# Picking the sixteen stand-in experts of a gate: an eight-largest search with replacement instead of a comparison of all pairs

## The reference, cut to what matters

```python
seq_rep = mean(hidden, axis=1)                 # (16, 512)
affinity = normed(seq_rep) @ normed(sim_matrix)  # (16, 32)
logits = affinity - sigmoid(gates)
gated = relu(logits)
mask = gated > 0
inactive = sum(mask, axis=1) == 0              # a row with no active expert
_, fb_idx = top_k(logits, 16)                  # its sixteen stand-ins
fb_mask = sum(one_hot(fb_idx, 32), axis=1)
mask = where(inactive, max(mask, fb_mask), mask)
routing = softmax(where(mask > 0, gated, -FMAX))
```

## Time and profile before

| | |
|---|---|
| three runs | 1649.87, 1651.27 and 1651.45 us; median 1651.27 us |
| the profiled execution | 1654.6 us, of which its span (first to last instruction) is 1652.9 us |
| PE, DVE, POOL, ACT busy | 92%, 72%, 62% and 59% of the span |
| mean granted TensorE clock | 0.955 of full speed |
| gated mixture block | from 386.3 to 541.5 us of the span |

### The profile page before, as it was taken

How to read it: one execution, slowest core, us unless ns; L and a number is a source line. 1 busy time by engine, 2 the same in 40 slices (tenths; PEclk the granted TensorE clock), 3 DMA queues, 4 the chain that set the end, 5 groups by cost and what they waited for, 6 DMA issues and landing times.

```text
span 1652.9 us, 27994 instructions
## 1 busy us (share of the span) xinstructions
PE 1513.4 (92%) x8637; PEld 1045.7 (63%) x8637; DVE 1194.2 (72%) x1863; ACT 980.0 (59%) x1527; POOL 1032.2 (62%) x855
## 2 busy tenths in 40 slices
PE   4999999997668599999999999886999999999996
PEld 3677777775434344444444444356899999899995
DVE  7688888888637567777777777256777777777774
ACT  6323333333624167888888887745767776677763
POOL 4788888884305478888888887601455555555553
PEclk9999999998879589999999999987999999999998
DMA  7344444446634857777876774292344444444443
GB/s 252 107 135 137 135 136 137 137 140 168 149 90 157 194 128 186 193 189 186 202 187 188 191 193 109 89 343 79 64 78 77 77 77 78 77 77 78 77 77 52
DMA packets 110841, 224.23 MB, mean 136 GB/s; under 512 B 12704, under 2 KB 12704, under 8 KB 109856
## 3 DMA queue, kind: packets, MB, share of 16 engines
q1 hardware_dynamic: 94848, 185.88, 40.0%
q0 software_dynamic: 15904, 37.23, 13.0%
HBM read 146.71 MB, written 75.84 MB: 135 GB/s over the span
## 4 chain that ended last, share of the span: by engine, by line
PE 41%; DMA 19%; issue 3%; DVE 2%; ACT 1%; POOL 1%; SPq 0%; POOLq 0%; DVEq 0%; ACTq 0%
DMA out_rows<-XN,slots 17%; PE pB L1426 10%; PE pO L1436 8%; PE pA L1408 8%; PE pA L1580 4%; PE pO L1449 4%; PE pO L1592 4%; DMA XN<-normed_rows,slots 1%; PE pO L1562 1%; PE pB L1417 1%; PE pA L1570 1%; PE pA L1498 1%; POOL out_rows L1392 1%; DVE low L1772 1%; DMA qs<-q_low 0%
## 5 line engine op out<-in xcount | busy, mean ns | idle before, releaser
L1772 DVE TENSOR_REDUCE low<-pA 128x2 f32<-128x1024 f32 x256 | 307.7, 1224 | 119.8 <-PE pA L1408 105.6
L1665 ACT ACTIVATE pt<-pB 128x512 f32<-128x512 f32 x512 | 287.9, 594 | 93.3 <-PE pB L1426 85.5
L431 PE MATMUL y<-kv,toep 128*128 128x288 f32 x1280 | 327.8, 413 | 9.0 <-DVEq L63 5.8
L1392 POOL DMA_INDIRECT out_rows<-XN,slots x71 | 194.9, 2746 | 215.0 <-DMA out_rows<-XN,slots 171.6
L431 PEld LDWEIGHTS y<-kv,toep 128*128 128x128 f32 x1280 | 239.0, 191 | 97.6 <-DVEq L63 34.1
L1580 PEld LDWEIGHTS pA<-XN,fc 128*128 128x128 f32 x2272 | 265.9, 193 | 8.0 <-issue 2.7
L1580 PE MATMUL pA<-XN,fc 128*128 128x128 f32 x2272 | 266.8, 276 | 1.9 <-issue 1.0
L1426 PE MATMUL pB<-qs,ks 98*128 98x512 f32 x512 | 230.0, 453 | 2.7 <-ACT pt L1665 2.4
L1426 PEld LDWEIGHTS pB<-qs,ks 98*128 98x128 f32 x512 | 97.3, 192 | 192.8 <-ACT pt L1665 147.7
L1408 PE MATMUL pA<-ks,qs 96*128 96x512 f32 x512 | 191.6, 419 | 20.5 <-DMA qs<-q_low 19.0
L401 ACT ACTIVATE ym<-y 128x384 f32<-128x384 f32 (+1 forms) x128 | 52.6, 411 | 230.6 <-PE y L431 230.6
(11 more groups left out here) (281 smaller groups left out, 2388.2 us busy)
## 6 DMA issues: line engine op xcount, KB each, us to landing
ks<-ctx_high SPq DMA_DIRECT2D x64, 256.0 KB, 4.6
qs<-q_high SPq DMA_DIRECT2D x64, 256.0 KB, 6.3
kc<-in_ctx_conv SPq DMA_DIRECT2D x32, 384.0 KB, 5.3
XN<-in_x SPq DMA_DIRECT2D x16, 512.0 KB, 10.5
toep<-kernel_and_skip SPq DMA_DIRECT2D x32, 256.0 KB, 3.6
ct<-in_ctx SPq DMA_DIRECT2D x16, 512.0 KB, 6.4
ctx_high<-kh SPq DMA_DIRECT2D x16, 512.0 KB, 4.5
ctx_low<-kl SPq DMA_DIRECT2D x16, 512.0 KB, 5.1
```

The costliest lines, as they stand in the source:

```text
L431: m = pe.matmul(y[half].rearrange("p (l n) c -> p l n c", l=CB)[:, l, :, 0:PAIRS], toep[u][:, (l - s) * P:(l - s + 1) * P], kv[u][:, half, ...
L1392: pool.indirect_dma_start(out=out["out"], out_offset=bass.IndirectOffsetOnAxis(ap=slots[:, j:j + 1], axis=0), in_=ys[j % 2], in_offset=Non ...
L1665: act.activation(pt[s][:, h, :], bank(u, n), ACT.Exp, scale=SCALE1).then_inc(s_exp, 1)
L1772: dve.tensor_reduce(ap(low[u % 2], t % CB * NH + t // CB, [[NH, 2], [1, 1]]), pA[n % 2], op=ALU.max, axis=AX.X, negate=True).then_inc(s_re ...
```

## The change

The rank of all logits goes. In its place VectorE finds the eight largest of the 32 logits of each row (`max`), replaces these eight in a copy by the most negative number (`match_replace`), and does both once more on the copy. What is then equal to the most negative number is one of the sixteen largest. The tile `later` and its two POOL instructions go with it, and so does its share of `s_con`: PE waits for 4 instead of 5.

```diff
-            later, over, same = (WM[0:B].rearrange("p b k h -> p (b k h)")[:, n * E0 * E0:(n + 1) * E0 * E0]
-                                 .rearrange("p (e f) -> p e f", f=E0) for n in range(3))
+            best = [sb(st, f"best{i}", [B, 8]) for i in range(FALLBACK // 8)]
+            left = [sb(st, f"left{i}", [B, E0]) for i in range(FALLBACK // 8)]
...
-            CONS = 5 + 1 + HQ
+            CONS = 4 + HQ
...
-                pool.memset(later, 1.0).then_inc(s_con, 1)
-                pool.wait_ge(s_con, 5)
+                pool.wait_ge(s_con, 4)
...
-                    pool.wait_ge(s_con, 6 + g)
+                    pool.wait_ge(s_con, 5 + g)
...
-                    if j == 5:
-                        pool.wait_ge(s_ot, j + 1)
-                        pool.affine_select(out=later, in_=later, compare_op=ALU.is_gt, fill=0.0, base=0,
-                                           pattern=[[1, E0], [-1, E0]], channel_multiplier=0).then_inc(s_con, 1)
-                        pool.wait_ge(s_con, CONS)
...
-                pe.wait_ge(s_con, 5)
+                pe.wait_ge(s_con, 4)
...
                 dve.wait_ge(s_con, CONS)
-                mine = ap(t["logits"], 0, [[1, E0], [0, E0]])
-                other = ap(t["logits"], 0, [[0, E0], [1, E0]])
-                chain.inc(dve.tensor_tensor(over, other, mine, ALU.is_gt))
-                chain.link(dve.tensor_tensor(same, other, mine, ALU.is_equal))
-                chain.link(dve.tensor_tensor(same, same, later, ALU.mult))
-                chain.link(dve.tensor_tensor(over, over, same, ALU.add))
-                chain.link(dve.tensor_reduce(t["rank"], over, op=ALU.add, axis=AX.X))
-                chain.link(dve.tensor_scalar(t["rank"], t["rank"], float(FALLBACK), cnt, ALU.is_lt, ALU.mult))
+                values = t["logits"]
+                for n in range(FALLBACK // 8):
+                    chain.link(dve.max(best[n], values))
+                    chain.link(dve.match_replace(left[n], best[n], values, -FMAX))
+                    values = left[n]
+                chain.link(dve.tensor_scalar(t["rank"], values, -FMAX, cnt, ALU.is_equal, ALU.mult))
```

## The result

The changed kernel takes 1641.18 us (median of 8 runs, 1639.03 to 1643.39), the kernel before 1650.11 us beside it (8 runs, 1645.85 to 1651.45): a ratio of 0.995 with a 95% interval of 0.9938 to 0.9962. The kernel before alone varies from 1642.0 to 1655.8 us from one execution to the next, far more than its first three runs told. The later runs come from five chips, on which its mean was between 1647.5 and 1651.0 us, so a comparison across chips is less sure than its ± says.

What follows compares the result with a forecast made beforehand. DVE's gate chain was taken to bound the block's second half. The gate's -4.92 and POOL's -0.57 sum to -5.49 us, off the median 1651.27: 1645.8 us, 0.33% less, range 1643.7 to 1648.7.

Steps and rivals of the forecast that it cites:

- The bound: Around the gate, DVE's chain alone sets PE's restart; every microsecond saved there is one microsecond of the whole.
- The search: At the gate, two searches and two replacements take 1.20 us instead of 6.12, saving 4.92 us (between 1.2 and 5.3).
- POOL's part: In the block's first loop, dropping the triangle's memset and select gains 0.57 us, between 0 and 0.6.
- The two waits of 0.29 and 0.28 us: DVE's waits before the third and fourth tiles' L821 in the first loop, expected to go, 0.57 us in all.
- a sign of being wrong: A first loop that ends where it did, instead of 0.57 us earlier.
- The fifth step: TensorE's clock behind the gate: the same 5.7 us from restart to rise expected, 2 us either side, worth 1.0 us.
- two places behind the gate: Mixing w_o after PE's restart, up to 1.0 us either way, and two rounds of `inner` at 499.98, 1.4 us.
- Rival (c): The clock's rise shifts at one or both places behind the gate, giving 1643.4 or 1648.2 us; chance 0.12.
- its own range: 1644.6 to 1647.2 us for the whole kernel: search 0.80 to 1.61, POOL 0 to 0.6, clock half a microsecond each way.

## Why the prediction was wrong in size and right in direction

- **The bound.** Right: DVE's chain alone set the restart of PE, w_o was long there, and what the gate gave arrived at the block's end. PE's idle time fell by 5.13 us with the chain, and the attention did not get longer.
- **The search.** Right, and sized well: 0.99 us for four operations against 1.20 counted (bounds 0.80 to 4.90). It was 0.22 us from start to start for a search and 0.28 for a replacement, of which 0.08 is the load of the eight values. The Trainium skill's page "VectorE: DVE Perf Modes", section "Two Vector instructions with no wait between them", counts a replacement as two instructions, and the trace agrees. Its advice on few operations ("Rules for kernel authors") is no bound here: six instructions replaced five and took 5.13 us less.
- **POOL's part.** This is the step that failed. The two waits of 0.29 and 0.28 us went as foretold, but the cap, "No more than these waits can be won: 0.57 us", did not hold: taking the triangle away measures 2.2 ± 0.5 us over four comparisons (1.7 ± 0.4 with the two runs that only move the memset), against 0.57. In the first pair of profiles the loop did not even end earlier, which the prediction had named as a sign of being wrong. The working looked at DVE's waits beside the memset only, as if the rest of the loop could not feel it.
- **The clock.** The fifth step, which weighed the clock, looked at two places behind the gate and took both at nothing. Rival (c), chance 0.12, had them move, and in the first pair of profiles both did: the rise came 4.4 us behind the restart instead of 5.8, and the rounds of `inner` took 3.67 us instead of 5.32. Over all profiles the two are worth 0.5 ± 0.5 us. The step put the first loop at nothing without a look, though there the length goes from 52.7 to 60.0 us with the time at the low clock. With the pauses of start and loop filled, old and new loops are alike (52.9 and 53.0) and the distance is the counted one within its error; this makes the clock the likely carrier of what POOL's part gave beyond the count, but does not show it.
- **The range.** It was centred on the median of three runs, 1651.27, where the 72 later ones have a mean of 1649.5. Of the 4.6 us between 1645.8 and 1641.2, 1.8 are this offset and 0.2 the search. The remaining 2.6 were not in the sum; by the four comparisons 1.6 of them belong to POOL's part and 0.7, with an error near 0.5, to the gate beyond its 5.13. (The lower end of its own range, 1644.6, should by its own terms be 1651.27 - 5.32 - 0.60 - 0.50 = 1644.85.)

What is not settled is how POOL's memset and select act on the clock. In the profiles with the memset ahead of PE's product the clock reached 2.4 GHz 7.6 to 8.4 us behind the block's start (six profiles, the one of the kernel before among them), without it 4.1 to 5.7 us in most (8.9 in one execution of the change). Filling only that pause in the old kernel brought the rise to 4.3 us, but the time down by 0.8 ± 1.2 us, which excludes neither nothing nor all. Whether the falls later in the loop became rarer, too, can't be told from one profile for each kernel: the loop is 57.8 ± 0.6 us long on average in the six with the memset ahead, and 56.9 ± 0.8 in the eight without it and without fillers.

## What to carry to other kernels

A comparison of all pairs on one short row costs its elements, not its instructions: with a fixed part near 0.13 us and 1 ns for each element, replacing 5 x 1,024 elements by four operations of 32 is won by over 5 us, and a few instructions more, at 0.2 us each, would not have changed that. Where an engine whose granted clock changes waits in many short pauses, count what the clock does in every loop that ends up waiting for it, even if another engine looks like the pacemaker: read the waits at the loop's slow places, not at its fast ones. And take the spread of an unchanged kernel from more than three runs before a forecast of a third of a per cent.

## What the runs showed of the hardware that was not expected

- VectorE's search for the eight largest of 32 values on 16 partitions takes 0.18 us, as long as a reduction of the same size (0.17); the replacement is a load of 0.08 us and a pass of 0.16 to 0.17.
- Unchanged code takes 36.7 us in one execution and 21.5 in another to get from 1.2 to 2.4 GHz at the start of the attention, and its first unit is 4.8 us longer in the former. The six full kernels profiled ahead of the fillers have 46.5 us (two) or 50.2 to 51.2 us (four) for that unit. It is one part of the spread of the whole kernel, beside the first loop (52.7 to 60.0 us) and the blocks ahead of it, which end between 383.8 and 386.5 us.
- Products that nobody reads, put into TensorE's pauses, held its clock at 2.4 GHz from 389.0 us in the old kernel and 391.7 in the new to the end of the first loop, and were worth 7.0 and 5.0 us. In the full kernel the clock still fell once in that loop, for 3.4 us. The Trainium skill's page "TensorE: Matmul & The Clock Gate", section "What's actually happening", says that the low clock is the resting state and activity lifts it. The runs agree: in the gate of the old kernel it is at 0.50 throughout without fillers, and reaches 1.00 at 462.3 us with them. Lifting it where another engine sets the pace gave no gain clear of the noise (1.0 ± 1.2 us); it paid where PE was waited for.
